# A cross-attention block on one core: two projection steps moved between the last products, another buffer for transposes, and the second batch's layer-norm statistics behind the attention

## What is computed

```python
residual = hidden_states
x = layer_norm(hidden_states, ln1_w, ln1_b)
q, k, v = x @ q_w + q_b, enc @ k_w + k_b, enc @ v_w + v_b      # split into 16 heads
scores = einsum('bhqd,bhkd->bhqk', q, k) / sqrt(32)            # masked
out = einsum('bhqk,bhkd->bhqd', softmax(scores), v)
hidden = out @ cproj_w + cproj_b + residual
y = layer_norm(hidden, ln2_w, ln2_b)
y = gelu_tanh(y @ fc_w + fc_b)                                 # 2048 wide
return hidden + y @ proj_w + proj_b
```

## Time and profile before

| | |
|---|---|
| median of 3 runs | 771.61 us (769.97 to 775.69) |
| the profiled execution | 771.54 us |
| its span, first to last instruction | 769.7 us |
| mean granted TensorE clock in it | 0.993 |
| TensorE, VectorE, ScalarE, GpSimd busy | 729.8, 544.4, 401.5, 351.0 us |

### The profile page before, as it was taken

One profiled execution on the slowest core, in us unless ns is written; L12 is line 12 of the kernel. 1 busy time (PEld: TensorE's weight loads), 2 busy tenths in 40 slices (PEclk: granted clock), 3 DMA queues, 4 the chain that ended last, 5 costly groups with the idle time before them and its releaser, 6 DMA issues.

```text
span 769.7 us, 10364 instructions
## 1 busy us (share of the span) xinstructions
PE 729.8 (95%) x3568; PEld 497.8 (65%) x3568; DVE 544.4 (71%) x1071; ACT 401.5 (52%) x690; POOL 351.0 (46%) x241
## 2 busy tenths in 40 slices
PE   7999999989999999999999889999999989999998
PEld 5878886733344444344436768778777878868886
DVE  6773347788888888898695857677599457654474
ACT  4434241276766666666684635354556554454442
POOL 2644150078998788798574367000045167000030
PEclk9999999999999999999999989999999999999999
DMA  9756377597666784678836832134883452033362
GB/s 328 236 161 229 127 223 231 196 265 171 157 165 149 187 235 115 173 197 180 228 103 156 259 105 70 40 85 115 212 270 104 118 179 83 27 96 96 95 207 82
DMA packets 118196, 124.24 MB, mean 161 GB/s; under 512 B 41248, under 2 KB 66084, under 8 KB 118144
## 3 DMA queue, kind: packets, MB, share of 16 engines
q1 hardware_dynamic: 91888, 98.39, 45.1%
q10 hardware_dynamic: 26256, 25.19, 11.0%
HBM read 94.05 MB, written 29.37 MB: 160 GB/s over the span
## 4 chain that ended last, share of the span: by engine, by line
PE 75%; DVE 15%; ACT 5%; issue 3%; DMA 1%; SPq 1%; POOL 0%; ACTq 0%; DVEq 0%
PE ps L592 20%; PE ps L594 19%; PE ps L593 19%; DVE ps L1344 7%; PE ps L715 5%; PE ps L699 5%; PE ps L684 4%; PE ps L730 4%; DVE R L1546 2%; ACT Pt L960 1%; DVE BIG L1458 1%; DMA yt<-FU 1%; DVE mx L1344 1%; PE ps L652 1%; DVE R L1276 1%
## 5 line engine op out<-in xcount | busy, mean ns | idle before, releaser
L960 ACT ACTIVATE Pt<-ps 128x512 f32<-128x512 f32 x256 | 137.6, 597 | 72.4 <-PE ps L699 71.5
L699 PE MATMUL ps<-BIG 98*128 98x512 f32 x256 | 92.7, 439 | 3.5 <-ACT Pt L960 3.1
L1344 DVE CUSTOM_DVE_ANT_0 ps<-ps,FU 128x512 f32<-128x512 f32 x128 | 84.6, 722 | 14.9 <-PE ps L684 14.8
L1344 DVE CUSTOM_DVE_ANT_0 ps<-ps,BIG 128x512 f32<-128x512 f32 x128 | 84.6, 723 | 10.9 <-PE ps L684 10.7
L699 PEld LDWEIGHTS ps<-BIG 98*128 98x128 f32 x256 | 44.1, 188 | 67.5 <-issue 28.3
L1458 DVE TENSOR_TENSOR BIG<-RW,BIG 128x512 fp32r<-128x512 f32 x64 | 50.2, 784 | 49.4 <-ACT BIG L1061 49.3
L1061 ACT ACTIVATE BIG<-RW 128x512 fp32r<-128x512 f32 x64 | 40.3, 629 | 80.7 <-PE ps L594 79.8
L592 PE MATMUL ps<-BIG,HR 128*128 128x512 f32 x172 | 68.4, 397 | 5.2 <-DVE HR L1453 5.2
L994 ACT ACTIVATE BF<-BF,cols 128x512 f32<-128x512 f32 x48 | 34.5, 723 | 68.1 <-DVE BF L1447 29.5
L1800 POOL TENSOR_TENSOR R<-Pt 128x1024 f32<-128x1024 f32 x20 | 47.3, 2390 | 46.6 <-ACT Pt L960 46.6
L1739 POOL TENSOR_TENSOR R<-R,cbt 128x512 f32<-128x512 f32 x16 | 26.0, 1652 | 93.2 <-DMA R<-hd 93.2
(11 more groups left out here) (186 smaller groups left out, 1734.9 us busy)
## 6 DMA issues: line engine op xcount, KB each, us to landing
RW<-in_proj_w ACTq DMA_DIRECT2D x64, 256.0 KB, 2.6
BIG<-qs SPq DMA_DIRECT2D x62, 256.0 KB, 2.8
BIG<-ks SPq DMA_DIRECT2D x62, 256.0 KB, 3.1
ks<-BIG SPq DMA_DIRECT2D x32, 256.0 KB, 2.0
qs<-BIG SPq DMA_DIRECT2D x32, 256.0 KB, 5.5
R<-hd SPq DMA_DIRECT2D x20, 256.0 KB, 4.1
RW<-in_fc_w ACTq DMA_DIRECT2D x20, 256.0 KB, 3.0
R<-in_x SPq DMA_DIRECT2D x16, 256.0 KB, 5.4
```

What stands on the lines that cost most here:

```text
L699: eng.matmul(bk, K_[0:98, j, kc * 128:(kc + 1) * 128], Q_[0:98, j, :], start=True, stop=True).then_inc(S["p_ra"], 1)
L960: eng.activation(Pt[:, r, j % 2, :], bank(bank_a(("s2", i, j))), ACT.Exp, scale=SCALE).then_inc(S["a_ra"], 1)
L1344: eng.tensor_tensor_reduce(out=scores, in0=scores, in1=MASK[s // 4], scale=1.0, scalar=-3.4e38, op0=ALU.add, op1=ALU.max, accum_out=mx[:, ...
```

## The change

Eight edits, in the order of the diff:

- `second(n)`: for the second half, the three buffers of the projection weights lie elsewhere, and wait for the products' buffers there.
- `turned(b, c)`: R0 for columns 2 and 3 of all batches but the first; the waits of `y_block` follow.
- The statistics of batch 1's layer norm leave steps 58 to 62 of the attention loop and stand behind `front_low_part(0, 2)`; in front of its norms and transposes now stands the division of the last head group. GpSimd's `root(1, 5)` goes behind `out_low(14)`.
- SyncE loads the first "wr" weights behind `y_store(1)` and `y_load(1)` instead of ahead of them; in half 1 ScalarE issues these loads at p = 0 and 1 instead of 3 and 4.
- TensorE makes `cproj` of batch 3 for all columns at p = 3, two ahead of `fc_second` and behind `fc_first(0, 4)`.
- `y_affine(1)` and `block(0, n)` on VectorE, `block_high` and `rest_high` on ScalarE stand at earlier `p`, `front_low_part(0, 6)` and `(0, 7)` behind them.
- `pj` of the first two steps of each half stand between the last three products, one behind rest(7,7) and one behind rest(7,4).
- ScalarE's and VectorE's parts for these two steps move ahead by one place each, and the loads of their weights too.

```diff
@@ -109,7 +109,8 @@
...
 
-            return [BIG[:, 21504 + 1024 * (n % 3) + 512 * h:][:, 0:512] for h in range(2)]
+            base = (21504, 22528, 23552)[n % 3] if n < 32 else (19968, 21504, 18944)[n % 3]
+            return [BIG[:, base + 512 * h:][:, 0:512] for h in range(2)]
 
@@ -125,7 +126,7 @@
...
         def turned(b, c):
-            return R0[:, c % 2, :] if b == 1 and c >= 2 else FU[:, c % 2, :]
+            return R0[:, c % 2, :] if b and c >= 2 else FU[:, c % 2, :]
 
@@ -330,7 +331,6 @@
...
         FRONT_HIGH, FRONT_LOW = (56, 57), (57, 58)
-        Y2_STATS = (58, 59, 60, 61)
 
@@ -548,14 +548,12 @@
...
             load_weights(("wf", 7, 0))
-            for m in range(2):
-                for h in range(2):
-                    load_weights(("wr", m, h))
             for c in range(4):
...
             y_load(1)
-            for h in range(2):
-                load_weights(("wr", 2, h))
+            for m in range(3):
+                for h in range(2):
+                    load_weights(("wr", m, h))
             for c in range(4):
@@ -887,23 +885,30 @@
...
                         sums(NS - 1)
+                    if q == 0 and p == 3:
+                        pe.wait_ge("v_rb", NB)
+                        for c in range(2):
+                            cproj(3, c, range(4), bank(c)).then_inc(S["p_cp"], 1)
                     fc_second(q, p)
-                    if q == 0 and 2 <= p < 4:
-                        pe.wait_ge("v_rb", NB)
-                        for c in (2 * p - 4, 2 * p - 3):
+                    if q == 0 and p == 3:
+                        for c in range(2, 4):
                             cproj(3, c, range(4), bank(c)).then_inc(S["p_cp"], 1)
...
                         fc_rest(q, p + 1, 6)
+                    else:
+                        pj(32 * q)
                     fc_rest(q, p, 4)
...
                         fc_rest(q, p + 1, 5)
+                    else:
+                        pj(32 * q + 1)
                     fc_rest(q, p, 3)
...
                         fc_rest(q, p + 1, 7)
-                for n in range(32 * q, 32 * q + 32):
+                for n in range(32 * q + 2, 32 * q + 32):
                     pj(n)
@@ -1055,7 +1060,7 @@
...
                 if f < 3 and b % 2 == 0:
-                    act.wait_ge("p_p3", HF * (b // 2) + (7 if b else 6))
+                    act.wait_ge("p_p3", HF * (b // 2) + (7 if b and f == 2 else 6))
                 if n >= 3:
@@ -1192,46 +1197,44 @@
...
                         load_weights(("wf", HF + 5 + p, 0))
-                    if q and 3 <= p < 5:
+                    if q and p < 2:
                         for h in range(2):
-                            load_weights(("wr", HF + p - 3, h))
+                            load_weights(("wr", HF + p, h))
                     if q and 5 <= p < 7:
...
                         split_out(NS - 1)
-                    if q == 0 and p == 4:
-                        block_high(0, 0)
-                        block_high(0, 1)
+                    if q == 0 and 3 <= p < 5:
+                        block_high(0, 2 * p - 6)
+                        block_high(0, 2 * p - 5)
                     if q == 0 and p == 5:
-                        rest_high(0, 0)
-                        block_high(0, 2)
-                        block_high(0, 3)
-                    if q == 0 and p == 6:
                         block_high(0, 4)
-                    if q and p == 6:
-                        rest_high(1, 0)
-                rest_high(q, 1)
+                    if p == (4, 5)[q]:
+                        rest_high(q, 0)
+                    if p == (5, 7)[q]:
+                        rest_high(q, 1)
                 gelu_rest(q, 0, 22)
...
                             load_weights(("wr", HF * q + p + 4, h))
+                    if 5 <= p < 7:
+                        load_weights(("pj", 32 * q + 2 * p - 10, 0))
+                        load_weights(("pj", 32 * q + 2 * p - 9, 0))
                     gelu_rest(q, p, 21)
+                    if p == 6:
+                        second_high(32 * q)
+                        hidden_high(32 * q)
                     gelu_rest(q, p, 12)
...
                         rest_high(q, p + 3)
-                    if 5 <= p < 7:
-                        load_weights(("pj", 32 * q + 2 * p - 10, 0))
-                        load_weights(("pj", 32 * q + 2 * p - 9, 0))
                     if p + 1 < HF:
...
                     if p == 6:
-                        second_high(32 * q)
-                        hidden_high(32 * q)
-                second_high(32 * q + 1)
-                hidden_high(32 * q + 1)
+                        second_high(32 * q + 1)
+                        hidden_high(32 * q + 1)
                 for n in range(2, 32):
@@ -1281,14 +1284,16 @@
...
                     dve.wait_ge("v_nm", 16 + 4 * (b - 1) + c + 1)
-                if b == 1 and c >= 2:
-                    dve.wait_ge("p_sm", NS)
-                elif c >= 2:
-                    dve.wait_ge(f"d_ys{c - 2}", 64 * (b + 1))
+                if b == 3:
+                    dve.wait_ge(f"d_ys{c}", 64 * b)
                 elif b == 2:
                     dve.wait_ge("v_wr", 2 * HF)
-                elif b:
-                    dve.wait_ge(f"d_ys{c + 2}", 64 * b)
+                elif b == 1 and c >= 2:
+                    dve.wait_ge("p_sm", NS)
+                elif b == 1:
+                    dve.wait_ge(f"d_ys{c + 2}", 64)
+                elif c >= 2:
+                    dve.wait_ge(f"d_ys{c - 2}", 64)
                 else:
@@ -1531,10 +1536,6 @@
...
                     y_block(0, Y_BLOCKS.index(i))
-                if i in Y2_STATS:
-                    c = Y2_STATS.index(i)
-                    dve.wait_ge(f"d_h{c}", 32)
-                    statistics(LN[1], 1, 5, c)
                 if i in PIECES:
@@ -1553,10 +1554,6 @@
...
                     variances(0, 4)
-                if i == 62:
-                    for c in range(4):
-                        aggregate(1, 5, c)
-                    variances(1, 5)
                 if i == 45:
@@ -1580,35 +1577,40 @@
...
                         front_low_part(0, 2)
+                        for c in range(4):
+                            dve.wait_ge(f"d_h{c}", 32)
+                            statistics(LN[1], 1, 5, c)
+                        for c in range(4):
+                            aggregate(1, 5, c)
+                        variances(1, 5)
                         front_low_part(0, 3)
+                        divide_a(NS - 1)
+                        divide_b(NS - 1)
+                        divide_t(NS - 1)
+                        divide_c(NS - 1)
                         for c in range(4):
...
                             y_block(1, c)
-                        divide_a(NS - 1)
-                        divide_b(NS - 1)
-                        divide_t(NS - 1)
-                        divide_c(NS - 1)
                     if q == 0 and p < 4:
                         front_low_part(0, p + 4)
-                    if q == 0 and p == 2:
+                    if q == 0 and p == 1:
                         for k in range(4):
                             y_affine(1, k)
+                    if q == 0 and 1 <= p < 3:
+                        block(0, 2 * p - 2)
+                        block(0, 2 * p - 1)
                     if q == 0 and 3 <= p < 5:
...
                             eng.tensor_tensor(R2[:, c, :], bank(c), R2[:, c, :], ALU.add).then_inc(S["v_cp"], 1)
-                        block(0, 2 * p - 6)
-                        block(0, 2 * p - 5)
-                    if q == 0 and p == 5:
+                    if q == 0 and p == 3:
                         block_low(0, 0)
                         block_low(0, 1)
-                        rest_low(0, 0)
-                    if q == 0 and p == 6:
+                    if q == 0 and p == 4:
                         block_low(0, 2)
-                if q:
-                    rest_low(1, 0)
+                rest_low(q, 0)
                 rest_low(q, 1)
@@ -1619,13 +1621,16 @@
...
                         rest_low(q, p + 2)
+                    if p == 6:
+                        second_low(32 * q)
+                        hidden_low(32 * q)
                     add_c12(q, p)
...
                         add_c22(q, p + 1)
-                    if p >= HF - 2:
-                        second_low(32 * q + p - HF + 2)
-                        hidden_low(32 * q + p - HF + 2)
+                    if p == 6:
+                        second_low(32 * q + 1)
+                        hidden_low(32 * q + 1)
                 for n in range(2, 32):
@@ -1805,8 +1810,8 @@
...
                     root(0, 4)
+            out_low(NS - 2)
             root(1, 5)
-            out_low(NS - 2)
 
```

## The result

The changed kernel takes 782.2 us (median of 4, 779.78 to 783.34) against 773.58 for the kernel before on the same chip: ratio 1.0124, 95% interval 1.0094 to 1.0154. It is slower by 1.2%; the prediction had said 771.3 (764 to 777) and gave "slower" a chance of 0.07. The profiled execution took 781.1 us.

What follows compares the result with a forecast made beforehand. TensorE was taken as the bound (matmul row busy 729.8 of 769.7 us), so only its idle or low-clock time could change. Terms -3.6 + 2.2 + 3.4 - 1.0 - 1.25 = -0.25 gave 771.3 us, range 764 to 777.

Steps and rivals of the forecast that it cites:

- the first front part: Half 0's front, up to the third product: idle about the same but in shorter pieces; -1.0 us, bounds -2.5 and +1.5.
- the other buffer: Before pj(19): R0 removes the 2.65 us stop for stores and the clock loss; -3.6 us, bounds -4.5 and -1.
- the second front: Second half's front: first product 2.5 us earlier, third at 623.1 instead of 624.37; -1.25 us, bounds -2.5 and 0.
- the two `pj`: Last products of each half: pj(2) idles 3.38 us; +2.2 in all, plus clock +3.4 (1.7 twice, bounds 0 and +6).
- `rest_low(0, 0)` ends at 444.1: First front part, VectorE: this end time, then rest_low(0, 1) at 446.7 and the third product at about 447.4.
- a clock that stays up from 447 to 453: Behind the first front part: no stop as long as 2.65 us, so 24 matmuls instead of 14 done by 453.
- the forecast's own prices (-2.3 and +1): First front part's clock, 447 to 453: -2.3 us if it stays up, +1 if it drops.
- What is late next: Behind pj(19): y_load(3) leaves only about 1.1 us earlier, so pj(24) starts about 0.7 us late.
- `add_u2` was to come at 622.4: Second half's front: add_u2 at 622.4 instead of 623.35, behind rest_high(1, 1) ending near 621.2 and rest_low(1, 1).
- The rivals: Gaps filled: 760.9 (0.12); stops don't lower clock: 767.9 (0.2); long stretch both times: 773.7 (0.15); late transposes: 779.2 (0.07).
- The late transposes decide: First front part: y_load(1) lands 4 us later than 427, holding front_low(6) and TensorE; 779.2 us, chance 0.07.

Runs made afterwards that it cites:

- r_gpsimd_waits: Changed kernel with the first two product weights loaded ahead of batch 1's stores and GpSimd's block_low(0, 3), (0, 4) waiting for rest_low(0, 1): 775.19 us, 1.0046 against before.
- q_two_pj_fixed: Kernel before plus two pj between each half's last products, pj(2)'s halves ahead of gelu12(7) on ScalarE and add_c12(7) on VectorE: 769.62 us, ratio 0.9965.
- p_two_pj: Kernel before with only pj(0) and pj(1) put between each half's last products, and their ScalarE and VectorE parts moved: 776.65 us, ratio 1.0058.
- q_light_bias: Kernel before with the other buffer for transposes of batches 2 and 3, and only 8 of 512 columns of the second output batch's bias added: 768.29 us (one run).
- t_rest_high: Changed kernel with all mends, statistics back in steps 58 to 61, and rest_high(1, 1) ahead of the second front's last gelu11: 759.93 us, 0.9849 against before.
- p_buffer: Kernel before with only the other buffer for the transposes of batches 2 and 3: 771.07 us, ratio 0.9974.
- q_early_loads: Changed kernel with SyncE's loads of the first two product weights ahead of batch 1's stores: 779.76 us, ratio 1.0114 against before.
- r_best_so_far: Kernel before plus other buffer, transposes two pj steps earlier, two pj with pj(2) mended, and changed second front; first front part as before: 762.62 us, ratio 0.9895.
- s_all_stats: Changed kernel with early weight loads, GpSimd's block_low wait, pj(2) mended, transposes two steps earlier, and statistics back in steps 58 to 61: 760.78 us, 0.9850 against before.

## Why the prediction was wrong

The sum said -0.25 us and TensorE's lateness came out at +9.5. Of these 9.75 us the first front part has 5.7, the other buffer 3.4 and the second front 0.75; the two `pj` missed by 0.1.

**The first front part (-1.0 forecast, +4.7 measured): the failing step.** The working was right up to `front_low(6)`: `y_load(1)` at 423.77 (424.1 forecast), `y_affine` from 426.5 to 430.2 (427.0 to 430.7), and `front_low(6)` ended at 433.83 (433.75). Then "`rest_low(0, 0)` ends at 444.1" came at 449.97. I had priced every instruction of VectorE behind `front_low(6)` as if GpSimd were silent, though the diff put GpSimd's weight sums behind `y_load(1)` and so beside VectorE's fullest stretch (431.52 to 442.95, with `block_low` on GpSimd right behind them to 448.55). From 430 on the working had 4.7 us of stops, the last 0.5 long; measured were 0.75, 1.51, 2.86 and 3.80, so 8.9. Before, the sums had run while VectorE was busy for only half of the time (a window of before: us, busy by engine in the page's order):

```profile
421.00:427.50 6.50, 6.50 (x31) 5.37 (x30) 3.28 (x4) 1.81 (x3) 6.22 (x9) 1.00 0.81 241
```

Only `rest_low(0, 1)` was taken "beside GpSimd". Part of the 2.86 is not the collision but an order: `rest_high(0, 1)` on ScalarE waited 1.15 us for the last of the late sums, and the last copy stood behind it. With GpSimd's sums early and its `block_low` late (r_gpsimd_waits) that same working is met: `rest_low(0, 0)` ends at 444.46 and the third product starts at 447.36, against 444.1 and 447.4. A row had a hint: at 424.01 three `y_affine` beside GpSimd took 2.84 us, 0.95 each, where a single one later takes 0.55.

**The clock behind it.** +4.7 compares two single executions. In the profiled execution of the kernel before, the clock was low for 6.8 us around the third product (446.3 to 453.1; the earlier trace rows has 6.0 of them); in the seven experiments that keep the first front part of before it was low for 3.4 us or not at all. From the front's start to the full stream these took 49.1 to 50.1 us, that execution of before 51.5, and the changed kernel 55.7. So the +4.7 has luck in it: against the seven this part costs 5.6 to 6.6 us. The forecast's -1.0 leaned on a clock that stays up from 447 to 453; it was low from 450.4 to 453.8. By the forecast's own prices (-2.3 and +1) this explains at most 2.0 of the 5.7 us.

**The two `pj` (+2.2 and +3.4 forecast, +5.5 measured): right.** The stops were 3.39 and 3.38 us (3.38 forecast), at 515.75 and 692.44, released by `hidden_low`; +1.1 each by lateness. The clock took 1.5 and 1.7 (1.7 forecast). The order of the queues was the cause, as q_two_pj_fixed shows: against p_two_pj it changes only the place of `pj(2)`'s parts on ScalarE and VectorE.

**The other buffer (-3.6 forecast, -0.2 measured): right mechanism, wrong end.** The stop at `pj(19)` went, and TensorE gained 4.5 us by `pj(20)` (4.49 forecast). The wait for `y_load(3)` at `pj(24)` cost 0.8 (0.7 forecast). What failed is that I stopped following the chain there. Behind `y_load(3)` in SyncE's queue stand the store of the output and the residual load, and behind those GpSimd's bias additions. These did not come earlier with TensorE (582.77 after, 8.2 later than before, with TensorE 3.6 to 4 later), and so fell on VectorE's differences when VectorE had no lead left: 3.1 us from `pj(26)` to `pj(28)`, lower clock included. That GpSimd's additions are the cause is shown by q_light_bias. "What is late next" was asked once; the second answer was the one that cost.

**The second front (-1.25 forecast, -0.5 measured): mis-sized.** `add_u2` was to come at 622.4 in the time of before; measured from the front's start it came 0.13 us earlier, not 0.95. The forecast knew that `rest_high(1, 1)` stood behind the last gelu; it put its end, and the low part behind it, too early. ScalarE and VectorE in the changed kernel:

```profile
627.18 0.69 ACT L999 ACTIVATE BF<-ps,cols 128x512 f32<-128x512 f32 x1 [1.18 <-PE ps L592]
627.76 0.41 ACT L1055 ACTIVATE BIG<-V 128x256 fp32r<-128x256 f32 x1
...
629.15 1.23 DVE L1393 TENSOR_TENSOR BIG<-R,BIG 128x1024 fp32r<-128x1024 f32 x1 [0.52 <-ACT BIG L1057]
```

In t_rest_high that gelu no longer stands ahead of it, and the stop goes.

**The rivals.** "The late transposes decide" gave 779.2, near the measured time, for a reason that was not there: `y_affine` was not late (426.5, 427.0 forecast), and r_gpsimd_waits rules it out, where y came later still and the products 5.5 us earlier. That it came near is luck. None of my rivals had two engines slowing each other, nor a gain given back, and the range held neither.

## What to carry to other kernels

When an edit moves work of one engine, lay its new stretch beside the fullest stretch of the engine that it may slow: here VectorE's instructions with two inputs in SBUF took 1.4 to 6 times as long beside GpSimd's (1.22 to 1.76 us, 0.42 to 2.56), and moving only one of the colliding pieces moved the collision. When a stop goes, follow every chain that does not move with the engine it held (here stores, loads, bias additions) to its end, not to the next wait. A piece of work put between two dependent steps covers a wait only if its successor's inputs do not stand in a queue behind that same wait.

## What the runs showed of the hardware that I had not expected

Two engines slowed each other by up to most of an instruction of the other. A VectorE `tensor_tensor` of 128x1024 with both inputs in SBUF took 1.22 us alone, 1.76 beside GpSimd's 128x256 instructions (0.74 alone, up to 1.76 then; changed kernel), and 3.15 on average beside its 128x1024 ones (2.4; q_early_loads). One of 128x512 took 0.69 alone and 1.75 beside the bias additions (p_buffer).

The lower clock does not follow the length of the stop. In p_buffer a stop of 1.93 us before 440.23 was followed by it; in r_best_so_far one of 3.61 us before 447.45 was not. The window of p_buffer, then the stop and the window of r_best_so_far:

```profile
440.40:443.70 3.30, 3.30 (x8) 2.57 (x9) 0.62 (x1) 1.91 (x4) 3.30 (x2) 0.50 0.97 372
```

```profile
447.45 0.47 PE L593 MATMUL ps<-SLX,BIG 128*128 128x512 f32 x1 [3.61 <-DVE BF L1432]
...
447.40:452.00 4.60, 4.55 (x20) 3.83 (x21) 2.16 (x4) 1.38 (x3) 4.44 (x7) 1.00 0.07 23
```

And most of the spread of one kernel's times goes with it. Of 81 executions of the kernel before, 73 have one of five mean granted clocks: 1.000 with 768.9 us on average (3 executions), 0.998 with 770.2 (18), 0.996 with 771.7 (28), 0.993 with 773.3 (13), 0.991 with 774.3 (11). The changed kernel ran at 0.987 to 0.993, s_all_stats at 0.999 to 1.000. From this, some 3 of s_all_stats's 11.6 us are clock; that is an estimate, the 771.7 less the 768.9 above. The page "TensorE: Matmul & The Clock Gate" (section "What's actually happening") of the Trainium skill says that the moment of the switch differs from run to run. The trace agrees: the kernel before and the seven kernels with its first front part had 6.8, 3.4 or 0 us of lower clock there.
